# Layer 3's cross pass: output matrix as two float32r parts in products of 512 columns, and a new task order

## The chip, the cores and the metric

One core of one Trainium2 chip. The metric is the device time of one launch in microseconds, the median of several runs. In this profile TensorE is PE (its weight loads PEld), VectorE is DVE, ScalarE is ACT, GpSimd is POOL, SyncE is SP.

## What is computed

A four-layer network on X of 16 batches x 128 tokens x 256 features, each layer an attention and a feed-forward part. Only layer 3's attention is touched. It has two passes, one over the batch's own tokens ("own") and one over a context ("cross"), and both do this (shortened from the reference; `wproj` has 2 x 2048 rows, half for each pass):

```
q = _ln(fp8_linear(ln_out, wqx, ...).reshape(b, s, g, hpg, d), qxln_w, qxln_b)
k, v = cond @ w_kv_x.T, split;  k = _ln(k, kxln_w, kxln_b)
o = _gqa(q, k, v)                      # 16 heads of 128, softmax over 128 keys
y = fp8_linear_pertensor(o * smooth, wproj)
x = x + y
```

The output projection rounds its input to FP8 values first. These have few bits, so they are exact in bfloat16 and in float32r alike. The matrix `wproj` is full float32, and so it is cut into parts that add up to it.

## The kernel before

`Layer3Pass.run` (L2388) writes one pass for one batch as some 85 tasks, and `CROSS_ORDER` (L2363) is a hand-written list of them: (group, task, number). Each engine walks the list and issues only the tasks that are its own, in that order (`steps`, L2488). An engine is in order: a task that waits for a semaphore holds all that stand behind it. One walk of the list, a *step*, works on four batches at once: group "a" (attention and output) on batch b, "c" (centre and turn heads) on b+1, "p" (project) on b+2, "r" on b+3. There are 14 walks with all or nearly all groups, two without "p", of which the last has "a" alone, and three shorter ones ahead that fill the pipeline.

The tasks of group "a", for units u = 0 to 3 of four heads each, and their engines:

- scores (PE, L2650) into the only score tile `s_ps`; maximum (DVE, L2860) reads it; exponential (ACT, L2723) reads it again and frees it; scores u+1 waits for exponential u.
- normalise (DVE, L2864), turn (PE, L2663), turned (ACT, L2757), apply (PE, L2670), scale (ACT, L2762).
- round (DVE, L2873): five instructions over 128x512, all bfloat16. The last, L2882, writes `catq`.
- output (PE, L2678): for each of four heads three products of 128x256, the heads' `catq` stationary, one for each bfloat16 part of the matrix (`wparts`), all added up in `o_ps[:, 0:256]`.
- add (DVE, L2884), once a batch: X += o_ps * scale.

Group "p": project 0 to 5 (PE, `product` L2597, float32r, 512 columns), keep (ACT, L2733), statistics (DVE, L2830), and at the end deviation (DVE, L2835) and inverse (POOL, L2546), which give mean and inverse deviation. Deviation waits until POOL has centred the batch before. Group "c": project and keep values (PE, ACT), center (POOL, L2554, four heads each, five of the six units), center here (DVE, L2852, the sixth), turn 0 to 5 (PE, L2632), affine (ACT, L2746).

The three bfloat16 parts are cut once, in the pass's fill (`cut_output`: ACT L2776, DVE L2894): four casts on ACT and four subtractions on DVE, by turns.

```
for p in range(PARTS):                                                    # L2686
    mm = nc.tensor.matmul(o_ps[:, 0:D], catq[:, u % 2, h, :], wparts[:, p, 4 * u + h, :], ...)
...
v.tensor_tensor(flat(catq[:, u % 2, :, :]), c16, m, ALU.subtract).then_inc(catq_ready, 1)   # L2882
```

Of the kernel before, what the change touches and what calls it, by code (L numbers as in the profile page):

```python
# [22 lines left out]
P = 128  # L23
# [2306 lines left out]
class Layer3Pass:  # L2330
# [35 lines left out]
        ("r", "value", 0), ("a", "scores", 1), ("a", "maximum", 1), ("c", "keep values", 1), ("a", "turn", 0),  # L2366
        ("a", "exponential", 1), ("c", "center here", 2), ("p", "project", 0), ("p", "keep", 0),
# [20 lines left out]
    def run(self):  # L2388
# [7 lines left out]
        with Stage(nc, self.name) as st:  # L2396
# [31 lines left out]
            weights = sb("weights", [P, 2, 4, P])  # L2428
            probst = sb("probst", [P, 2, 4, P])
# [3 lines left out]
            catq = sb("catq", [P, 2, 4, P], BF16)  # L2433
            wparts = sb("wparts", [P, PARTS, 16, D], BF16)
# [79 lines left out]
            with nc.Block() as block:  # L2514
# [72 lines left out]
                def _(pe):  # L2587
# [90 lines left out]
                    def output(b, u):  # L2678
                        pe.wait_ge(catq_ready, at_batch(b, U, u + 1))
                        if u == 0:  # L2680
                            wait(pe, added, at_batch(b, 1, 0))
                            if b == 0:

                                pe.wait_ge(part_left, 4)
                        for h in range(4):
                            for p in range(PARTS):  # L2686
# [13 lines left out]
                def _(act):  # L2700
# [45 lines left out]
                    def affine_task(b, m):  # L2746
                        if isinstance(b, int) and b == 0 and m == 0:

                            act.wait_ge(part_left, 4)
# [26 lines left out]
                    def cut_output():  # L2776
                        act.wait_ge(wproj_in, 16)
                        for p in range(2):
# [22 lines left out]
                def _(dve):  # L2801
# [82 lines left out]
                    def add(b, k):  # L2884
                        dve.wait_ge(multiplied, at_batch(b, U, U))
                        v.scalar_tensor_tensor(cols(self.X, b), o_ps[:, 0:D], out_scale[:, 0:1], cols(self.X, b),
                                               ALU.mult, ALU.add).then_inc(added, 1)
# [6 lines left out]
                    def cut_output():  # L2894
                        for p in range(2):
# [183 lines left out]
```

## Time and profile before

| | |
|---|---|
| median of 3 runs | 3121.82 us (3118.33 to 3124.68) |
| the profiled execution | 3118.86 us, its span 3117.0 us |
| mean granted TensorE clock | 0.886 of full |
| cross pass of layer 3 | from 2103.0 us (first DMA) to 2576.4 us |
| busy in the span | PE 2380.8 us, DVE 1739.0, ACT 1320.1, POOL 1169.4 |

Busy is the union of an engine's instructions. A PE product goes on for a while after the next has begun, so its busy time covers short stalls; DVE instructions also overlap a little at their ends, and between dependent ones lies a short pipeline gap that counts as neither busy nor, in the timeline, as a wait. The number in brackets at the end of a timeline row is the idle time before it, and what ended it.

### The profile page before, as it was taken

The page shows a single profiled execution, that of the slowest core. Times are in us where ns is not written, and L with a number is a line of the kernel's source. Part 1 is how long each engine was busy: PE and PEld are TensorE (multiplying, and loading weights), DVE is VectorE, ACT ScalarE, POOL GpSimd, SP SyncE. Part 2 cuts the span into 40 slices and gives each one's busy share as a digit, 9 for nine tenths or more (in the row PEclk, how much of TensorE's full clock was granted, in tenths as well). Part 3 has the DMA queues.
Part 4 walks back from the last instruction along what each step waited for, and adds up shares of the span by engine and source line. Part 5 has one row for each costly group of instructions (what it writes and reads, how often), then busy time and mean ns, then how long its engine had stood idle before and what let it go on. Part 6 is the DMA issues. An engine that isn't in the chain of part 4 may idle for free. (4 is left out here: it accounts for less than half of the span.)

```text
span 3117.0 us, 45806 instructions
## 1 busy us (share of the span) xinstructions
PE 2380.8 (76%) x14906; PEld 1740.0 (56%) x14906; DVE 1739.0 (56%) x3738; ACT 1320.1 (42%) x3059; POOL 1169.4 (38%) x1183
## 2 busy tenths in 40 slices
PE   4887043955988577479558888877999983999997
PEld 2332022433546333367447777766888873777876
DVE  4775585645444155233368888866888864233232
ACT  0667151740200145211167777765788761111110
POOL 4541003510002242130167777736888851500000
PEclk9999565986989789789779999988999986999999
DMA  5232102532210323200110000011000001200001
GB/s 124 69 86 57 39 0 71 152 101 101 115 53 0 69 66 90 66 18 1 35 61 1 0 0 0 1 41 39 5 5 5 2 1 75 59 1 1 1 1 27
DMA packets 85673, 127.72 MB, mean 41 GB/s; under 512 B 20203, under 2 KB 66827, under 8 KB 81803
## 3 DMA queue, kind: packets, MB, share of 16 engines
q1 hardware_dynamic: 85515, 125.67, 14.1%
q8 instruction: 92, 1.51, 0.2%
q14 instruction: 66, 0.54, 0.1%
HBM read 75.99 MB, written 11.14 MB: 28 GB/s over the span
## 5 line engine op out<-in xcount | busy, mean ns | idle before, releaser
L478 DVE TENSOR_REDUCE a_mraw<-a_first_ps 128x4 f32<-128x1024 f32 (+1 forms) x256 | 310.7, 1222 | 148.0 <-PE a_first_ps L329 147.6
L386 ACT ACTIVATE a_et<-a_second_ps 128x1024 f32<-128x1024 f32 x256 | 262.1, 1024 | 160.6 <-PE a_second_ps L347 158.4
L2558 POOL TENSOR_SCALAR a3x_raw<-a3x_raw,a3x_mu,a3x_dev 128x128 f32<-128x128 f32 x320 | 281.7, 892 | 5.3 <-issue 5.3
L1451 DVE TENSOR_TENSOR f3e_gated<-f3e_silu,f3e_u_ps 128x512 f32<-128x512 f32 x96 | 66.1, 688 | 304.1 <-PE f3e_s_ps L1402 299.2
L2558 POOL TENSOR_SCALAR a3o_raw<-a3o_raw,a3o_mu,a3o_dev 128x128 f32<-128x128 f32 x256 | 232.0, 917 | 4.8 <-issue 4.8
L1432 ACT ACTIVATE f3e_silu<-f3e_g_ps 128x512 f32<-128x512 f32 x96 | 57.4, 598 | 396.1 <-PE f3e_g_ps L1389 396.1
L1411 PE MATMUL f3e_y_ps<-f_w,f3e_hidden 128*128 128x256 f32 x768 | 181.4, 380 | 0.0
L364 PE MATMUL a_o_ps<-a_et,a_vt 128*32 128x256 f32 x2048 | 168.0, 400 | 7.3 <-ACT a_osb L416 6.1
L347 PE MATMUL a_second_ps<-a_qs,a_ks 64*128 64x256 bf16 (+2 forms) x896 | 117.8, 298 | 63.7 <-ACT a_et L386 54.1
L1411 PEld LDWEIGHTS f3e_y_ps<-f_w,f3e_hidden 128*128 128x128 f32 x768 | 146.6, 191 | 18.4 <-DVE f3e_hidden L1454 1.2
L329 PE MATMUL a_first_ps<-a_ks,a_qs 64*128 64x256 bf16 (+2 forms) x1280 | 123.6, 268 | 19.1 <-DMA a_ks<-a_parts 10.4
L347 PEld LDWEIGHTS a_second_ps<-a_qs,a_ks 64*128 64x128 bf16 (+1 forms) x896 | 42.0, 96 | 163.2 <-ACT a_et L386 127.9
L2728 ACT ACTIVATE a3x_weights<-a3x_s_ps,a3x_nmax 128x128 f32<-128x128 f32 x256 | 91.1, 377 | 60.4 <-DVE a3x_nmax L2862 60.4
L1371 POOL CAST f_w_high<-f_w_raw 128x512 fp32r<-128x512 f32 x36 | 25.0, 694 | 238.2 <-SPq L1350 220.3
L2728 ACT ACTIVATE a3o_weights<-a3o_s_ps,a3o_nmax 128x128 f32<-128x128 f32 x256 | 93.1, 412 | 27.5 <-DVE a3o_nmax L2862 27.1
L2549 POOL TENSOR_TENSOR a3o_dev<-a3o_var,a3o_minus_half 128x24 f32<-128x24 f32 x16 | 69.0, 4310 | 94.8 <-DVE a3o_var L2850 94.8
L1362 POOL CAST f_x_high<-f_xnt 128x1024 fp32r<-128x1024 f32 x9 | 9.3, 1038 | 252.7 <-PE f3e_s_ps L1402 175.1
L2687 PE MATMUL a3o_o_ps<-a3o_wparts,a3o_catq 128*128 128x256 bf16 x768 | 101.9, 286 | 0.6 <-DVE a3o_catq L2882 0.6
L2606 PE MATMUL a3x_p_ps<-a_wkv,a3x_ctx_parts 128*128 128x512 f32 x384 | 102.1, 409 | 0.0
L2606 PE MATMUL a3o_p_ps<-a_wq,a3o_xq 128*128 128x512 f32 x256 | 80.6, 441 | 27.5 <-ACT a3o_vv L2743 16.8
L329 PEld LDWEIGHTS a_first_ps<-a_ks,a_qs 64*128 64x128 bf16 (+1 forms) x1280 | 72.0, 101 | 45.8 <-issue 16.1
L2687 PE MATMUL a3x_o_ps<-a3x_wparts,a3x_catq 128*128 128x256 bf16 x768 | 94.2, 273 | 0.7 <-DVE a3x_catq L2882 0.7
(537 smaller groups left out, 6380.4 us busy)
## 6 DMA issues: line engine op xcount, KB each, us to landing
f_w<-in_f_w SPq DMA_DIRECT2D x16, 1216.0 KB, 8.5
a_qs<-a_parts SPq DMA_DIRECT2D x144, 128.0 KB, 2.4
a_ks<-a_parts SPq DMA_DIRECT2D x96, 128.0 KB, 2.4
f_w_raw<-in_f_w SPq DMA_DIRECT2D x25, 256.0 KB, 2.6
a_od<-a_osb SPq DMA_DIRECT2D x64, 64.0 KB
a_oc<-a_od SPq DMA_DIRECT2D x16, 256.0 KB, 2.8
a_zr<-a_zd SPq DMA_DIRECT2D x64, 64.0 KB
a_od<-a_osb SPq DMA_DIRECT2D x8, 512.0 KB, 3.3
```

What stands on the lines that cost most here:

```text
L329: last = nc.tensor.matmul(self.first_ps[:, g % 2, u, c * N:c * N + N], self.queries(p, self.ROWS, b, tq, rows), self.keys(p, self.ROWS, b, ...
L347: last = nc.tensor.matmul(out, self.keys(p, self.ROWS_WITH_MAXIMA, b, t, rows), self.queries(p, self.ROWS_WITH_MAXIMA, b, tq, slice(0, N)) ...
L364: last = nc.tensor.matmul(self.o_ps[32 * j:32 * j + 32, columns], self.vt[:, b // 2 % self.NV, b % 2, c, self.block(k, j), :], self.et[:, ...
L386: self.nc.scalar.activation(self.et[:, g % self.WAVES_HELD, :, :], self.second_ps[:, :, :], ACT.Exp, scale=self.scale).then_inc(self.e_rea ...
L478: v.tensor_reduce(out, self.first_ps[:, g % 2, :, :].rearrange("p u (c n) -> p u c n", n=N), AX.X, ALU.max).then_inc(self.max_taken, 1)
L1411: last = nc.tensor.matmul(y_ps[:, k, 0:D], hidden[:, t % 2, k * P:k * P + P], self.w2[:, t, :], start=(t == 0), stop=(t == L - 1))
L1451: nc.vector.tensor_tensor(gated[:, t % 2, :], silu[:, t % 2, :], u_ps[:, :], ALU.mult).then_inc(gated_ready, 1)
L2549: nc.gpsimd.tensor_tensor(dev[:, :], var[:, :], minus_half[:, :], ALU.pow)
L2558: mm = nc.gpsimd.tensor_scalar(head, head, mu[:, h:h + 1], dev[:, h:h + 1], ALU.subtract, ALU.mult)
L2606: mm = nc.tensor.matmul(out, lhs, rhs, start=(i == 0), stop=(i == len(pairs) - 1))
L2687: mm = nc.tensor.matmul(o_ps[:, 0:D], catq[:, u % 2, h, :], wparts[:, p, 4 * u + h, :], start=(u == 0 and h == 0 and p == 0), stop=(u == U ...
L2728: mm = nc.scalar.activation(weights[:, u % 2, h, :], s_ps[:, h, :], ACT.Exp, bias=nmax[:, u % 2, h:h + 1], accum_out=total[:, u % 2, h:h + 1])
```

## The change

In the cross pass alone (the own pass keeps its code):

- The matrix is kept as two float32r parts side by side, `whalves` (128 x 16 x 2 x 256), in place of `wparts` of three bfloat16 parts. ACT copies (rounds) it in two halves, DVE subtracts in two halves.
- `catq` becomes float32r. Its four other rounding tiles stay bfloat16.
- output: for each head one product of 512 columns, high part into `o_ps[:, 0:256]`, low part into `o_ps[:, 256:512]`.
- add: two additions to X, with a drain between them.
- `weights` and `probst` move into `wraw`, the buffer that the own pass loaded weights through, which is free by then.
- `CROSS_ORDER` is another.

```
-            catq = sb("catq", [P, 2, 4, P], BF16)
-            wparts = sb("wparts", [P, PARTS, 16, D], BF16)
+            catq = sb("catq", [P, 2, 4, P], BF16 if own else F32R)
+            if own:
+                wparts = sb("wparts", [P, PARTS, 16, D], BF16)
+            else:
+                whalves = sb("whalves", [P, 16, 2, D], F32R)
+            LEFT = 4 if own else 2
...
                         for h in range(4):
+                            if not own:
+                                mm = nc.tensor.matmul(o_ps[:, :], catq[:, u % 2, h, :],
+                                                      whalves[:, 4 * u + h, :, :].rearrange("p k n -> p (k n)"),
+                                                      start=(u == 0 and h == 0), stop=(u == U - 1 and h == 3))
+                                continue
...
                     def cut_output():
                         act.wait_ge(wproj_in, 16)
+                        if not own:
+                            for h in range(2):
+                                nc.scalar.copy(whalves[:, 8 * h:8 * h + 8, 0, :], wproj[:, 8 * h:8 * h + 8, :]
+                                               ).then_inc(part_taken, 1)
+                            return
...
                     def add(b, k):
                         dve.wait_ge(multiplied, at_batch(b, U, U))
+                        if not own:
+                            v.scalar_tensor_tensor(cols(self.X, b), o_ps[:, D:2 * D], out_scale[:, 0:1], cols(self.X, b),
+                                                   ALU.mult, ALU.add)
+                            v.drain()
                         v.scalar_tensor_tensor(cols(self.X, b), o_ps[:, 0:D], out_scale[:, 0:1], cols(self.X, b),
                                                ALU.mult, ALU.add).then_inc(added, 1)
...
                     def cut_output():
+                        if not own:
+                            for h in range(2):
+                                dve.wait_ge(part_taken, h + 1)
+                                v.tensor_tensor(whalves[:, 8 * h:8 * h + 8, 1, :], wproj[:, 8 * h:8 * h + 8, :],
+                                                whalves[:, 8 * h:8 * h + 8, 0, :].bitcast(F32),
+                                                ALU.subtract).then_inc(part_left, 1)
+                            return
```

What the new list does to the engines is seen best in a step written out behind the loop. POOL's and SP's rows are the same before and after.

PE, from the first output task (`o_ps`) of a step to the second scores (`s_ps`) of the next. Here `t_ps` is a turn of four heads, `av_ps` apply, `p_ps` with `ctx_parts` projection of keys or values. Before:

```order
L2687 MATMUL a3x_o_ps<-a3x_wparts,a3x_catq 128x256 x12
L2674 MATMUL a3x_av_ps<-a3x_probst,a3x_vv 128x256 x2
L2687 MATMUL a3x_o_ps<-a3x_wparts,a3x_catq 128x256 x12
L2647 MATMUL a3x_t_ps<-a3x_ident,a3x_raw 128x128 x8
L2687 MATMUL a3x_o_ps<-a3x_wparts,a3x_catq 128x256 x12
L2647 MATMUL a3x_t_ps<-a3x_ident,a3x_raw 128x128 x4
L2687 MATMUL a3x_o_ps<-a3x_wparts,a3x_catq 128x256 x12
L2659 MATMUL a3x_s_ps<-a3x_qk 128x128 x4
L2606 MATMUL a3x_p_ps<-a_wkv,a3x_ctx_parts 128x512 x12
L2659 MATMUL a3x_s_ps<-a3x_qk 128x128 x4
```

After:

```order
L2694 MATMUL a3x_o_ps<-a3x_whalves,a3x_catq 128x512 x4
L2654 MATMUL a3x_t_ps<-a3x_ident,a3x_raw 128x128 x4
L2681 MATMUL a3x_av_ps<-a_wraw,a3x_vv 128x256 x2
L2694 MATMUL a3x_o_ps<-a3x_whalves,a3x_catq 128x512 x4
L2654 MATMUL a3x_t_ps<-a3x_ident,a3x_raw 128x128 x8
L2694 MATMUL a3x_o_ps<-a3x_whalves,a3x_catq 128x512 x4
L2654 MATMUL a3x_t_ps<-a3x_ident,a3x_raw 128x128 x8
L2694 MATMUL a3x_o_ps<-a3x_whalves,a3x_catq 128x512 x4
L2666 MATMUL a3x_s_ps<-a3x_qk 128x128 x4
L2613 MATMUL a3x_p_ps<-a_wkv,a3x_ctx_parts 128x512 x12
L2666 MATMUL a3x_s_ps<-a3x_qk 128x128 x4
```

Twelve products of 256 columns are four of 512, and one turn moved behind the third output task. Ahead of these rows, the other applies and projections stand earlier than before.

DVE, from the add of a batch over maximum 0, normalise 0 and so on to the statistics of units 0 and 1. Before:

```order
L2886 SCALAR_TENSOR_TENSOR X<-a3x_o_ps,a3x_out_scale,X 128x256
...
L2862 TENSOR_REDUCE a3x_nmax<-a3x_s_ps 128x4
L2866 RECIPROCAL a3x_inv_total<-a3x_total 128x4
L2869 TENSOR_TENSOR a3x_weights<-a3x_weights,a3x_inv_total 128x512
L2862 TENSOR_REDUCE a3x_nmax<-a3x_s_ps 128x4
L2857 TENSOR_SCALAR a3x_raw<-a3x_raw,a3x_mu,a3x_dev 128x128 x4
L2866 RECIPROCAL a3x_inv_total<-a3x_total 128x4
L2869 TENSOR_TENSOR a3x_weights<-a3x_weights,a3x_inv_total 128x512
L2862 TENSOR_REDUCE a3x_nmax<-a3x_s_ps 128x4
L2833 BN_STATS a3x_stats<-a3x_raw 128x6 x8
```

After:

```order
L2904 SCALAR_TENSOR_TENSOR X<-a3x_o_ps,a3x_out_scale,X 128x256
L2907 SCALAR_TENSOR_TENSOR X<-a3x_o_ps,a3x_out_scale,X 128x256
...
L2879 TENSOR_REDUCE a3x_nmax<-a3x_s_ps 128x4
L2883 RECIPROCAL a3x_inv_total<-a3x_total 128x4
L2886 TENSOR_TENSOR a_wraw<-a_wraw,a3x_inv_total 128x512
L2879 TENSOR_REDUCE a3x_nmax<-a3x_s_ps 128x4
L2874 TENSOR_SCALAR a3x_raw<-a3x_raw,a3x_mu,a3x_dev 128x128 x4
L2883 RECIPROCAL a3x_inv_total<-a3x_total 128x4
L2886 TENSOR_TENSOR a_wraw<-a_wraw,a3x_inv_total 128x512
L2879 TENSOR_REDUCE a3x_nmax<-a3x_s_ps 128x4
L2850 BN_STATS a3x_stats<-a3x_raw 128x6 x8
```

Nothing is moved in this stretch; one addition is new.

DVE, later in the step, from the end of round 0 to the start of the next one. Before:

```order
L2882 TENSOR_TENSOR a3x_catq<-a3x_cat,a3x_cmagic 128x512
L2866 RECIPROCAL a3x_inv_total<-a3x_total 128x4
L2869 TENSOR_TENSOR a3x_weights<-a3x_weights,a3x_inv_total 128x512
L2833 BN_STATS a3x_stats<-a3x_raw 128x6 x4
L2268 TENSOR_SCALAR a3x_cat<-a3x_cat 128x512
```

After:

```order
L2899 TENSOR_TENSOR a3x_catq<-a3x_cat,a3x_cmagic 128x512
L2850 BN_STATS a3x_stats<-a3x_raw 128x6 x8
L2883 RECIPROCAL a3x_inv_total<-a3x_total 128x4
L2886 TENSOR_TENSOR a_wraw<-a_wraw,a3x_inv_total 128x512
L2268 TENSOR_SCALAR a3x_cat<-a3x_cat 128x512
```

Statistics 3 and 4 now stand ahead of normalise 3, and rounds 1, 2 and 3 follow on each other with nothing between them (before, statistics 4 stood between rounds 1 and 2).

## Rows read from the trace of the kernel before

**Rows 1.** Window of 27 us in the middle of the cross pass.

```profile
core 0: us, PE busy (x) PEld busy (x) DVE busy (x) ACT busy (x) POOL busy (x), PEclk, DMA share, GB/s
2300.00:2327.00 27.00, 26.98 (x182) 23.15 (x181) 21.81 (x70) 21.56 (x69) 22.95 (x24) 1.00 0.02 5
```

**Rows 2.** Timeline of PE in one step: start us, us, instructions.

```profile
2301.94 1.47 PE L2687 MATMUL a3x_o_ps<-a3x_wparts,a3x_catq 128*128 128x256 bf16 x12
2303.25 1.03 PE L2674 MATMUL a3x_av_ps<-a3x_probst,a3x_vv 128*128 128x256 f32 x4
...
2321.80 1.64 PE L2606 MATMUL a3x_p_ps<-a_wkv,a3x_ctx_parts 128*128 128x512 f32 x6
2323.27 1.03 PE L2674 MATMUL a3x_av_ps<-a3x_probst,a3x_vv 128*128 128x256 f32 x4
```

**Rows 3.** Timeline of DVE, one step from add to add (its waits).

```profile
2310.56 0.48 DVE L2886 SCALAR_TENSOR_TENSOR X<-a3x_o_ps,a3x_out_scale,X 128x256 f32 x1
...
2313.33 0.18 DVE L2866 RECIPROCAL a3x_inv_total<-a3x_total 128x4 f32<-128x4 f32 x1 [1.57 <-ACT a3x_weights L2728]
...
2314.54 0.69 DVE L2862 TENSOR_REDUCE a3x_nmax<-a3x_s_ps 128x4 f32<-128x512 f32 x1 [0.27 <-PE a3x_s_ps L2659]
...
2316.81 0.18 DVE L2866 RECIPROCAL a3x_inv_total<-a3x_total 128x4 f32<-128x4 f32 x1 [0.39 <-ACT a3x_weights L2728]
...
2318.02 0.69 DVE L2862 TENSOR_REDUCE a3x_nmax<-a3x_s_ps 128x4 f32<-128x512 f32 x1 [0.27 <-PE a3x_s_ps L2659]
...
2329.53 0.38 DVE L2268 TENSOR_SCALAR a3x_cat<-a3x_cat 128x512 bf16<-128x512 bf16 x1 [0.34 <-ACT a3x_cat L2767]
...
2332.14 0.41 DVE L2268 TENSOR_SCALAR a3x_cat<-a3x_cat 128x512 bf16<-128x512 bf16 x1 [0.32 <-ACT a3x_cat L2767]
...
2333.45 0.79 DVE L2878 TENSOR_TENSOR a3x_cat<-a3x_cat,a3x_cmagic 128x512 bf16<-128x512 bf16 x1
...
2335.70 0.20 DVE L2839 TENSOR_TENSOR a3x_mu<-a3x_stats 128x24 f32<-128x24 f32 x1 [0.16 <-issue]
...
2337.33 0.48 DVE L2886 SCALAR_TENSOR_TENSOR X<-a3x_o_ps,a3x_out_scale,X 128x256 f32 x1
```

**Rows 4.** Groups of DVE by line, cross pass (busy us, mean ns, idle before).

```profile
L2869 DVE TENSOR_TENSOR a3x_weights<-a3x_weights,a3x_inv_total 128x512 f32<-128x512 f32 x64 | 44.6, 697 | 4.8
L2882 DVE TENSOR_TENSOR a3x_catq<-a3x_cat,a3x_cmagic 128x512 bf16<-128x512 bf16 x64 | 29.1, 454 | 4.8
```

**Rows 5.** Groups of DVE by shape, whole span: a subtraction with mixed types, one without.

```profile
L1747 DVE TENSOR_TENSOR f0h_scaled<-f0h_scaled,f0h_magic 128x2048 f32<-128x2048 f32 x8 | 18.3, 2292 | 0.6
L1750 DVE TENSOR_TENSOR f0h_hid<-f0h_scaled,f0h_magic 128x2048 bf16<-128x2048 f32 x8 | 18.3, 2292 | 0.8
```

**Rows 6.** Timeline of POOL in one step.

```profile
2288.76 17.80 POOL L2558 TENSOR_SCALAR a3x_raw<-a3x_raw,a3x_mu,a3x_dev 128x128 f32<-128x128 f32 x20 [0.19 <-issue]
2306.54 0.78 POOL L2576 TENSOR_TENSOR a3x_ctx_parts<-a3x_ctxs,a3x_ctx_parts 128x256 fp32r<-128x256 f32 x1
2310.65 4.19 POOL L2549 TENSOR_TENSOR a3x_dev<-a3x_var,a3x_minus_half 128x24 f32<-128x24 f32 x1 [3.33 <-DVE a3x_var L2850]
```

**Rows 7.** Timeline of DVE and POOL in the pass's fill.

```profile
2121.83 4.53 DVE L2899 TENSOR_TENSOR a3x_qk<-a3x_qk,a3x_wparts 128x2048 f32<-128x2048 f32 x2
2126.28 4.52 DVE L2899 TENSOR_TENSOR a3x_wparts<-a3x_qk,a3x_wparts 128x2048 bf16<-128x2048 f32 x2
...
2122.00 6.16 POOL L2549 TENSOR_TENSOR a3x_dev<-a3x_var,a3x_minus_half 128x24 f32<-128x24 f32 x1 [11.63 <-DVE a3x_var L2850]
...
2128.84 17.60 POOL L2558 TENSOR_SCALAR a3x_raw<-a3x_raw,a3x_mu,a3x_dev 128x128 f32<-128x128 f32 x20 [0.19 <-issue]
```

**Rows 8.** Timeline of PE: scores 0 and 1 of the first step and of the last two.

```profile
2147.41 1.92 PE L2659 MATMUL a3x_s_ps<-a3x_qk 128*128 128x128 f32 x8
...
2522.45 1.06 PE L2659 MATMUL a3x_s_ps<-a3x_qk 128*128 128x128 f32 x8
...
2550.42 1.06 PE L2659 MATMUL a3x_s_ps<-a3x_qk 128*128 128x128 f32 x8
```

More of the change, by code:

```diff
@@ L2365 @@
         ("c", "keep values", 0), ("a", "normalise", 0), ("c", "center", 0), ("c", "project values", 1),
-        ("r", "value", 0), ("a", "scores", 1), ("a", "maximum", 1), ("c", "keep values", 1), ("a", "turn", 0),
-        ("a", "exponential", 1), ("c", "center here", 2), ("p", "project", 0), ("p", "keep", 0),
[14 rows of a table removed]
+        ("r", "value", 0), ("a", "scores", 1), ("a", "maximum", 1), ("c", "keep values", 1), ("p", "project", 0),
+        ("a", "exponential", 1), ("c", "center here", 2), ("a", "turn", 0), ("p", "keep", 0), ("a", "normalise", 1),
[14 rows of a table added]
     ]
@@ L2427, in run @@
             inv_total = sb("inv_total", [P, 2, 4])
-            weights = sb("weights", [P, 2, 4, P])
-            probst = sb("probst", [P, 2, 4, P])
+            if own:
+                weights = sb("weights", [P, 2, 4, P])
+                probst = sb("probst", [P, 2, 4, P])
+            else:
+                weights, probst = (mats.wraw[:, k, :].rearrange("p (u h n) -> p u h n", u=2, h=4) for k in range(2))
             cat16 = sb("cat16", [P, 2, 4, P], BF16)
@@ L2432, in run @@
             cmagic = sb("cmagic", [P, 4, P], BF16)
-            catq = sb("catq", [P, 2, 4, P], BF16)
-            wparts = sb("wparts", [P, PARTS, 16, D], BF16)
+            catq = sb("catq", [P, 2, 4, P], BF16 if own else F32R)
+            if own:
+                wparts = sb("wparts", [P, PARTS, 16, D], BF16)
+            else:
+                whalves = sb("whalves", [P, 16, 2, D], F32R)
+            LEFT = 4 if own else 2
             wproj = qk[:, :, :, :].rearrange("p h k n -> p (h k n)")[:, 0:16 * D].rearrange("p (k n) -> p k n", k=16)
@@ L2682, in output @@
                             if b == 0:
-                                pe.wait_ge(part_left, 4)
+                                pe.wait_ge(part_left, LEFT)
                         for h in range(4):
+                            if not own:
[3 more added lines that the diff above has]
+                                continue
                             for p in range(PARTS):
@@ L2747, in affine_task @@
                         if isinstance(b, int) and b == 0 and m == 0:
-                            act.wait_ge(part_left, 4)
+                            act.wait_ge(part_left, LEFT)
                         act.wait_ge(heads_turned, at_batch(b, L, m + 1))
```

28 rows, old and new, of the table CROSS_ORDER are left out of this document.

## Prediction

> **What bounds the kernel now.** I read four views of the cross pass: windows, PE's timeline, DVE's timeline with the waits in it, and POOL's timeline. Only this pass changes. From scores 0 of its first step to scores 0 fourteen steps later pass 2522.45 - 2147.41 = 375.0 us, so a step takes 26.8 us [rows 8].
>
> The window [rows 1] seems to answer at once: PE is busy 26.98 of 27 us at full granted clock (2.4 GHz), weight loads 23.15, DVE 21.8, ACT 21.6, POOL 23. But PE's busy time includes the tail of each product, so a stall of a few tenths does not show in it. The reader should therefore ask a second question of each engine: if PE were free at once, how short could a step be? For DVE the timeline answers it [rows 3]. From add to add pass 26.77 us, and the waits in between are seven: 1.57 (normalise 0 for exponential 0), 0.27 (maximum 1 for scores 1), 0.39 (normalise 1 for exponential 1), 0.27 (maximum 2 for scores 2), 0.34 and 0.32 (rounds 2 and 3 for ACT's scale), 0.16 (deviation). Sum 3.32. All the rest, 23.45 us, is DVE's own work with its pipeline gaps.
>
> Four of these waits are not PE's doing. There is one score tile: maximum u, exponential u, scores u+1, maximum u+1 follow on each other, and DVE has nothing in its order to put in the holes but what is there now. 1.57 + 0.27 + 0.39 + 0.27 = 2.50 us stay however fast PE becomes. With the 0.16 that makes a ring through DVE of 23.45 + 2.66 = 26.11 us. Before the change DVE is thus within 0.66 us a step of being the bound: PE can give back two waits, 0.34 + 0.32, and no more.
>
> POOL's ring is shorter: 4.19 for the power, about 0.7 to the first centre (as in the fill, from 2128.16 to 2128.84), 17.80 for twenty centres [rows 6, 7], and DVE's deviation 2337.33 - 2335.70 = 1.63 [rows 3]: 24.3 us. It waits 3.33 us for DVE.
>
> **The change part by part, for a step.**
>
> Output products. An output task holds PE from 2301.94 to 2303.25, 1.31 us for twelve of 256 columns. A float32r product of 512 columns with a new stationary each time is there too: six take 2323.27 - 2321.80 = 1.47, so 0.245 each and four 0.98 [rows 2]. PE is relieved of 4 x (1.31 - 0.98) = 1.32 us a step. On the path lies of this only what DVE waited for, at most 0.66.
>
> Task order. On PE, applies and projections stand earlier, so ACT's scale is earlier. On DVE the stretch from add to the statistics of units 0 and 1 is the same, so the four waits of 2.50 remain. Later, rounds 1, 2, 3 stand together behind normalise 3, with two statistics ahead of it: 1.6 us of work that moved in front. Both let the scales be ready when the rounds come. I take the whole 0.66 as gained. The bound from below for this term is 0 (the waits stay), and nothing else in DVE's order is removed.
>
> The second addition. It reads PSUM like the present one: 0.48, and with the drain that holds the next about 0.56 [rows 3]. It stands at DVE's worst place: maximum 0 is queued behind it, exponential 0 waits for that, scores 1 for this, and with it PE. Nothing covers it: +0.56. Nothing in the timeline would let it be less.
>
> `catq` as float32r. This is a side effect of the type, four times a step: a subtraction of two bfloat16 tiles of 128x512 that writes 32-bit values. No row shows this mixture. The nearest below is the present one, all bfloat16: 0.43 in the timeline's rounds, mean 454 ns with a few held up. The nearest above is the same operation at the same width in float32: 0.69, mean 697 ns [rows 4]. What do mixed types take? At 2048 elements, a float32 subtraction takes 2292 ns with float32 output and 2292 with bfloat16 output [rows 5]: one 16-bit operand does not help where others are 32-bit. By this I take the upper end, 0.69, +0.26 each and +1.04 a step. The lower end is 0. The Trainium skill says the same of the unseen case: by "VectorE: DVE Perf Modes", section "What auto-detection actually checks", two elements a cycle need every tensor of a two-source operation to be 16-bit. If a 16-bit source were enough, against that page, this term would be nothing.
>
> So DVE's ring: 26.77 - 0.66 + 0.56 + 1.04 = **27.71 us**, +0.94 against now. PE then needs about 26.8 - 1.32 = 25.5 at most, POOL 24.3: both wait for DVE. PE will stand still behind scores 0 and the value projections until exponential 0 is done, about 1 us longer than now, and again ahead of some outputs for `catq`.
>
> Weight loads for 32-bit `catq` are longer than for bfloat16, but the 0.245 above is start to start with such loads. The move of `weights` and `probst` costs nothing: same shapes, same types, no wait added.
>
> Number of steps. Fourteen steps run at DVE's ring. The first is an exception: the clock is low at its start, and its scores take 1.92 instead of 1.06 us [rows 8], so PE holds part of it; I count it half. 13 x 0.94 + 0.5 = **+12.7**.
>
> The last two steps. In the one from 2522.45 to 2550.42 (27.97 us) the projections are absent. It ends on POOL's last centre (about 22.6 us after deviation's result) and then on output tasks behind turns. The new order puts only one turn and one output task, 0.44 + 0.98, behind that centre, where two output tasks at 1.31 stood. I take -2.0, between 0 and -3. The very last step: shorter output, longer last `catq` and the second addition: -0.33 + 0.26 + 0.56, about **+0.4**.
>
> The fill. Four subtractions of 2.26 us on DVE become two [rows 7], and two of ACT's casts go. The path there is POOL's: power from 2122.00, centres until 2146.4, scores at 2147.41 [rows 7, 8]. The power took 6.16 us beside the subtractions, 4.19 in the loop [rows 6]. With half of them gone I take **-0.7** (0 to -2.0). DVE's and ACT's other savings are covered by POOL's centres.
>
> Sum: 12.7 - 2.0 + 0.4 - 0.7 = **+10.4 us**. The profiled execution of 3118.86 would become 3129.3 (its span is 1.9 less). The median of the runs is 3.0 above that execution, so the median forecast is 3121.82 + 10.4 = **3132 us**.
>
> **The rivals.**
>
> 1. *PE is the bound, and DVE's holes shrink with it.* For it speaks the 26.98 of 27. Against it speak the four waits above, which end on ACT and on scores that were issued as soon as ACT was done. It would give -1.32 x 14 = -18.5, with the ends some -21: 3101 us. It decides if a step is nearer 25.5 than 26.8. The Trainium skill (its first page, "Trainium Kernel Development and Optimization", section "Performance Expectations") warns against reading matmul busy time as nearness to the limit; the weight loads, 23.15 of 27, agree with the warning. Chance 0.06.
>
> 2. *`catq` costs no more than now.* Then the ring is 26.77 - 0.66 + 0.56 = 26.67, -0.1 a step: -1.4, and with the ends' -2.0 + 0.1 - 0.7 it is -4: 3118 us. Deciding point: the mean duration of the last instruction of a round, 0.45 against 0.69. Chance 0.13.
>
> 3. *The order's gain does not come, or DVE and POOL get in each other's way.* A bfloat16 sum at 2333.45 took 0.79 where others take 0.52 [rows 3], at the time at which POOL subtracts in `ctx_parts` (26.64 us after 2306.54 [rows 6]). If such a meeting falls on every step anew it is +0.3 x 14 = +4. If the two waits of 0.66 remain it is +0.66 x 13 = +9. Together up to 3144, each alone 3136 to 3141. Chance 0.17.
>
> 4. *The change shortens nothing on PE*, since a product with both operands new runs at 0.3 or more. PE would still be at 26.7 and hidden by DVE's 27.7: the forecast's time. No chance of its own.
>
> **How the numbers follow.** A difference under 0.2% (6.2 us) can hardly be told from none here. The forecast, 0.64, spans about +4 to +15, from the bounds of its small terms; about a sixth of it lies under +6.2. Rival 2 has most of its chance within 0.2%, a little below. So: faster 0.09, same 0.21, slower 0.70. The range takes in the forecast, most of rival 2 and the single cases of rival 3: 3118 to 3140.
>
> **What would show it.** In the profile after: the last instruction of round at 0.69 instead of 0.43; two additions of 0.48; add to add 27.7 us; no wait of DVE for ACT's scale; still 1.57 ahead of normalise 0; PE's busy time at 25 to 26 of 27 with waits named ahead of scores 1 and output; POOL's wait ahead of its power grown from 3.3 to above 4 us. The prediction is wrong if a step is under 26.7 us: then either `catq` was cheap (its row tells), or the four waits did move with PE.

## The result and the profile after

The changed kernel takes 3130.69 us (median of 14 runs, 3123.89 to 3135.19), the kernel before 3122.82 (median of 14, 3118.33 to 3127.28). The ratio is 1.0025, 95% interval 1.0016 to 1.0033: 5 to 10 us slower. The profiled execution took 3130.35 us.

First the page's head. Beside before's numbers in the table above, PE has lost 12 us of busy time and DVE has gained 13.

```profile
span 3128.6 us, 44810 instructions
...
PE 2369.1 (76%) x14394; PEld 1712.2 (55%) x14394; DVE 1751.8 (56%) x3752; ACT 1316.7 (42%) x3057; POOL 1181.1 (38%) x1183
```

The window of one step in the middle of the pass, to be read beside [rows 1]:

```profile
2311.00:2338.00 27.00, 25.70 (x144) 20.97 (x144) 22.41 (x71) 20.89 (x68) 23.51 (x23) 1.00 0.02 5
```

PE was busy 26.98 of 27 us and now 25.70, at the same full clock: in equal windows it is busy 1.3 us less. A step is not such a window, since it has become longer. From add to add (mean of 13) PE's busy time falls from 26.52 to 25.79 us, by 0.73, and its idle time grows from 0.11 to 1.56. Where PE stands still is in its timeline of that step, in every step at the same two places: ahead of the last output task and ahead of scores 1.

```profile
2311.28 1.20 PE L2694 MATMUL a3x_o_ps<-a3x_whalves,a3x_catq 128*128 128x512 f32 x4 [0.59 <-DVE a3x_catq L2899]
2312.31 1.05 PE L2666 MATMUL a3x_s_ps<-a3x_qk 128*128 128x128 f32 x8
2313.12 3.04 PE L2613 MATMUL a3x_p_ps<-a_wkv,a3x_ctx_parts 128*128 128x512 f32 x12
2317.06 1.16 PE L2666 MATMUL a3x_s_ps<-a3x_qk 128*128 128x128 f32 x8 [0.90 <-ACT a_wraw L2740]
```

Output at 512 columns goes start to start in 1.03 us a task (2312.31 - 2311.28), where 1.31 was [rows 2] and 0.98 forecast.

DVE from add to add, the counterpart of [rows 3]:

```profile
2309.99 1.24 DVE L2899 TENSOR_TENSOR a3x_catq<-a3x_cat,a3x_cmagic 128x512 fp32r<-128x512 bf16 x1
...
2313.70 0.48 DVE L2904 SCALAR_TENSOR_TENSOR X<-a3x_o_ps,a3x_out_scale,X 128x256 f32 x1
2314.27 0.48 DVE L2907 SCALAR_TENSOR_TENSOR X<-a3x_o_ps,a3x_out_scale,X 128x256 f32 x1
2314.77 0.69 DVE L2879 TENSOR_REDUCE a3x_nmax<-a3x_s_ps 128x4 f32<-128x512 f32 x1
2317.04 0.18 DVE L2883 RECIPROCAL a3x_inv_total<-a3x_total 128x4 f32<-128x4 f32 x1 [1.57 <-ACT a_wraw L2740]
...
2318.25 0.69 DVE L2879 TENSOR_REDUCE a3x_nmax<-a3x_s_ps 128x4 f32<-128x512 f32 x1 [0.27 <-PE a3x_s_ps L2666]
...
2320.52 0.18 DVE L2883 RECIPROCAL a3x_inv_total<-a3x_total 128x4 f32<-128x4 f32 x1 [0.50 <-ACT a_wraw L2740]
...
2321.74 0.69 DVE L2879 TENSOR_REDUCE a3x_nmax<-a3x_s_ps 128x4 f32<-128x512 f32 x1 [0.16 <-PE a3x_s_ps L2666]
...
2328.03 0.70 DVE L2899 TENSOR_TENSOR a3x_catq<-a3x_cat,a3x_cmagic 128x512 fp32r<-128x512 bf16 x1
...
2332.74 0.70 DVE L2899 TENSOR_TENSOR a3x_catq<-a3x_cat,a3x_cmagic 128x512 fp32r<-128x512 bf16 x1
...
2335.05 0.70 DVE L2899 TENSOR_TENSOR a3x_catq<-a3x_cat,a3x_cmagic 128x512 fp32r<-128x512 bf16 x1
...
2337.35 1.24 DVE L2899 TENSOR_TENSOR a3x_catq<-a3x_cat,a3x_cmagic 128x512 fp32r<-128x512 bf16 x1
...
2341.07 0.48 DVE L2904 SCALAR_TENSOR_TENSOR X<-a3x_o_ps,a3x_out_scale,X 128x256 f32 x1
```

The reader should see four things. The wait of 1.57 ahead of normalise 0 stands as it was. Both waits for ACT's scale are gone. The last instruction of a round takes 0.70 and not 0.43. And one of the four takes 1.24. POOL's timeline tells what that one met:

```profile
2309.96 0.72 POOL L2583 TENSOR_TENSOR a3x_ctx_parts<-a3x_ctxs,a3x_ctx_parts 128x256 fp32r<-128x256 f32 x1
2313.78 4.18 POOL L2556 TENSOR_TENSOR a3x_dev<-a3x_var,a3x_minus_half 128x24 f32<-128x24 f32 x1 [3.10 <-DVE a3x_var L2867]
...
2318.91 18.44 POOL L2565 TENSOR_SCALAR a3x_raw<-a3x_raw,a3x_mu,a3x_dev 128x128 f32<-128x128 f32 x20 [0.57 <-issue]
2337.32 0.72 POOL L2583 TENSOR_TENSOR a3x_ctx_parts<-a3x_ctxs,a3x_ctx_parts 128x256 fp32r<-128x256 f32 x1
```

POOL's subtraction in `ctx_parts` starts at 2309.96 and 2337.32, DVE's slow `catq` at 2309.99 and 2337.35. Over the pass, the group of [rows 4]:

```profile
L2899 DVE TENSOR_TENSOR a3x_catq<-a3x_cat,a3x_cmagic 128x512 fp32r<-128x512 bf16 x64 | 51.2, 800 | 5.1 <-issue 0.4
```

**Where the time went.** I measure the pass from add to add.

| us | before | after | difference | forecast |
|---|---|---|---|---|
| pass start to the first add | 74.34 | 71.34 | -3.0 | -0.7 + 0.5 |
| 13 steps | 13 x 26.626 | 13 x 27.346 | +9.4 | +12.2 |
| last step but one | 27.11 | 25.16 | -1.95 | -2.0 |
| last step and what follows it | 25.79 | 27.16 | +1.4 | +0.4 |
| the pass | 473.4 | 479.2 | +5.8 | +10.4 |

The two profiled spans differ by 11.6 us, the pass by 5.8; the rest lies in stages that the change does not touch (the pass itself starts 2.2 us later). The medians differ by 7.9. The experiments below were each timed against the kernel before on the same chip (its medians there: 3122.57 for e1 to e4, 3123.30 for e5 to e7, 3123.53 for e8 to e10), and the pass of each was also measured in its trace, which leaves out the stages that no edit touches. One of e8's eleven runs took 5506.66 us, in a slow state, and is not in its ratio.

DVE's step, taken start to start over eight steps in the middle and grouped: additions 0.45 to 1.07; `catq` 1.55 to 3.02; the two scale waits, 0.65, gone; the other four instructions of a round, with statistics, maximum and centre, 0.85 less in all; everything else, the four waits that stay among it, 0.1 more. Sum 0.62 + 1.48 - 0.65 - 0.85 + 0.1 = +0.70, beside +0.71 over the same eight steps and +0.72 over 13.

### The profile page after: what moved, and what is told of

It is laid out like the page before. It is cut to its first block and busy times, and to the rows that moved or that the text cites. A ratio compares the mean times of both kernels' runs of the same rounds, so it can differ in the third digit from the quotient of the medians.

```text
span 3128.6 us, 44810 instructions
## 1 busy us (share of the span) xinstructions
PE 2369.1 (76%) x14394; PEld 1712.2 (55%) x14394; DVE 1751.8 (56%) x3752; ACT 1316.7 (42%) x3057; POOL 1181.1 (38%) x1183
## 5 line engine op out<-in xcount | busy, mean ns | idle before, releaser
L2565 POOL TENSOR_SCALAR a3x_raw<-a3x_raw,a3x_mu,a3x_dev 128x128 f32<-128x128 f32 x320 | 295.3, 935 | 5.3 <-issue 5.3
L329 PE MATMUL a_first_ps<-a_ks,a_qs 64*128 64x256 bf16 (+2 forms) x1280 | 122.1, 266 | 19.9 <-DMA a_ks<-a_parts 10.2
L2740 ACT ACTIVATE a_wraw<-a3x_s_ps,a3x_nmax 128x128 f32<-128x128 f32 x256 | 90.7, 368 | 76.0 <-DVE a3x_nmax L2879 76.0
L2666 PE MATMUL a3o_s_ps<-a3o_qk 128*128 128x128 f32 x512 | 74.3, 290 | 22.4 <-ACT a3o_weights L2740 21.6
```

The source lines that it names most:

```text
L329: last = nc.tensor.matmul(self.first_ps[:, g % 2, u, c * N:c * N + N], self.queries(p, self.ROWS, b, tq, rows), self.keys(p, self.ROWS, b, ...
L2565: mm = nc.gpsimd.tensor_scalar(head, head, mu[:, h:h + 1], dev[:, h:h + 1], ALU.subtract, ALU.mult)
L2666: mm = nc.tensor.matmul(s_ps[:, h, :], qk[:, q, 4 * u + h, :], qk[:, q, 16 + 2 * u + h // 2, :], start=True, stop=True)
L2740: mm = nc.scalar.activation(weights[:, u % 2, h, :], s_ps[:, h, :], ACT.Exp, bias=nmax[:, u % 2, h:h + 1], accum_out=total[:, u % 2, h:h + 1])
```

## The experiments

In each table row below: step is the mean of 13 steps add to add; "pass" its length.

| | median, ratio to before [95%] | pass | step |
|---|---|---|---|
| before | 3122.82 | 473.4 | 26.63 |
| after | 3130.69, 1.0025 [1.0016, 1.0033] | 479.2 | 27.35 |
| e1 order alone | 3124.92, 1.0007 [0.9998, 1.0016] | 472.5 | 26.61 |
| e2 products alone | 3133.32, 1.0038 [1.0027, 1.0050] | 482.7 | 27.34 |
| e3 one addition | 3121.45, 0.9999 [0.9990, 1.0008] | 469.0 | 26.70 |
| e4 half of `catq` | 3118.38, 0.9986 [0.9977, 0.9995] | 468.3 | 26.68 |
| e5 split moved | 3122.59, 0.9998 [0.9989, 1.0007] | 474.1 | 26.88 |
| e6 late additions | 3121.68, 0.9993 [0.9984, 1.0002] | 468.2 | 26.64 |
| e7 both | 3126.73, 1.0008 [0.9999, 1.0017] | 476.8 | 27.20 |
| e8 e6, last turn later | 3119.16, 0.9981 [0.9972, 0.9990] | 466.6 | 26.59 |
| e9 e8, split moved | 3116.56, 0.9977 [0.9968, 0.9986] | 466.6 | 26.51 |
| e10 e8 on old products | 3127.92, 1.0011 [1.0002, 1.0021] | 475.5 | 26.94 |

### e1: the new order on the old arithmetic

The kernel before, with the new `CROSS_ORDER`:

```
-        ("r", "value", 0), ("a", "scores", 1), ("a", "maximum", 1), ("c", "keep values", 1), ("a", "turn", 0),
+        ("r", "value", 0), ("a", "scores", 1), ("a", "maximum", 1), ("c", "keep values", 1), ("p", "project", 0),
...
```

> The kernel before with the new task list alone (bfloat16 parts, one addition). Theory (a ring through VectorE sets the step, and the order frees its two waits for the scales): the step falls from 26.66 us (add to add, mean of 13) to between 26.1, which is VectorE's ring without these waits, and 26.4, if TensorE's own work of some 26.0 us with small stalls takes over; time 3.5 to 8 us below before. Rival (TensorE is the bound and the products made the difference): no gain, 26.6 to 26.7, time within 2 us of before. Second rival (the order was only good together with short products): a longer step, 26.8 or more.

A miss: the step stays at 26.61, as before. Two scale waits of 0.34 and 0.32 have become one of 0.71, ahead of round 3 (DVE's timeline):

```profile
2334.37 0.43 DVE L2882 TENSOR_TENSOR a3x_catq<-a3x_cat,a3x_cmagic 128x512 bf16<-128x512 bf16 x1
2335.51 0.44 DVE L2268 TENSOR_SCALAR a3x_cat<-a3x_cat 128x512 bf16<-128x512 bf16 x1 [0.71 <-ACT a3x_cat L2767]
```

PE's idle time is 0.13 a step (0.11 in the kernel before). With two different orders PE has next to no idle time and the step is the same, so with twelve products PE is the limit, at 26.6, and DVE's scale waits are that limit as seen from DVE. What does come is 0.9 us in the step before the last.

### e2: the new products on the old order

The changed kernel, with the old `CROSS_ORDER` (the diff above the other way round).

> The changed kernel with the old task list. Theory: the ring through VectorE gets +0.57 for the second addition and +1.1 to +1.4 for the wider catq, and on the old list TensorE, relieved by 1.3 us, delivers the scales earlier too, so that most of the two waits goes without the new list: step 27.4 to 28.0, time 9 to 18 us above before. Rival (TensorE sets the step): 25.3 to 25.6, time 15 us or more below before. If the new list is what freed the waits, it is 27.9 or more; if not, within 0.2 of the changed kernel's 27.32.

The step is the changed kernel's to 0.01 us, and no scale wait is in it. So the products freed both waits and brought all of the loss per step, and the order brought nothing per step. The order is worth 3.5 us in the pass, at its end alone: the last step but one takes 27.04 here and 25.16 in the changed kernel, the last 27.89 against 26.12. `catq` has its 1.24 here too, once a step.

### e3: one addition

Each head's product split into two of 256 columns that add up in `o_ps[:, 0:256]`; the second addition and its drain go.

```
+                                for p in range(2):
+                                    mm = nc.tensor.matmul(o_ps[:, 0:D], catq[:, u % 2, h, :],
+                                                          whalves[:, 4 * u + h, p, :],
...
-                            v.scalar_tensor_tensor(cols(self.X, b), o_ps[:, D:2 * D], out_scale[:, 0:1], cols(self.X, b),
-                                                   ALU.mult, ALU.add)
-                            v.drain()
```

> The changed kernel with the two float32r parts summed in the same 256 columns of PSUM (eight products of 256 columns in each output task in place of four of 512) and so with one addition. Theory: the step loses the second addition, 0.57 us, and nothing else: 27.32 becomes 26.7 to 26.8, time about 8 us below the changed kernel, that is equal to before within 2 us; TensorE's output task may take up to 1.5 us with eight weight loads, and that must not show. Rival (TensorE matters): the longer output tasks give the gain back, step 27.2 or more.

The step loses 0.65, the pass 10.2 us. Eight products of 256 take PE no longer than four of 512:

```profile
2309.96 1.21 PE L2695 MATMUL a3x_o_ps<-a3x_whalves,a3x_catq 128*128 128x256 f32 x8 [0.58 <-DVE a3x_catq L2901]
```

The 0.65 is not the second addition alone. In this kernel POOL's subtraction meets `catq` 5 times in 64 and not 12, worth 0.27 a step over the eight middle steps; the additions take 0.54 less there, start to start; and other rows take 0.2 more. PE now waits for POOL's last centre, 1.1 us in every other step or 0.59 on the mean, where the changed kernel has no such wait.

So the wide product bought nothing here, and its price was the second addition. What PE gained, it gained from two float32r parts in place of three of bfloat16.

### e4: a shorter last instruction of round

The last instruction of a round writes 256 of the 512 columns, the rest of `catq` stays zero from the fill: half of the output projection is left out of the result. PE's work is the same.

```
-                        v.tensor_tensor(flat(catq[:, u % 2, :, :]), c16, m, ALU.subtract).then_inc(catq_ready, 1)
+                        n = 4 * P if own else 2 * P
+                        v.tensor_tensor(flat(catq[:, u % 2, :, :])[:, 0:n], c16[:, 0:n], m[:, 0:n],
+                                        ALU.subtract).then_inc(catq_ready, 1)
```

> The changed kernel, but the last instruction of a round writes the first 256 of 512 columns of catq alone; heads 2 and 3 of each unit stay zero, so half of the output projection is left out of the result, with all products still issued. Theory: the instruction takes about 0.42 us as the bfloat16 one did, in place of 0.69 and of 1.24 where it meets GpSimd's subtraction in ctx_parts, and the step loses 4 x 0.27 and some of the 0.54 of that meeting: 27.32 becomes 25.9 to 26.3, time 14 to 20 us below the changed kernel and 6 to 12 below before. Rival (the width of catq is covered by other waits): a step within 0.3 us of 27.3.

```profile
L2907 DVE TENSOR_TENSOR a3x_catq<-a3x_cat,a3x_cmagic 128x256 fp32r<-128x256 bf16 x64 | 27.8, 434 | 4.8
```

The instruction falls from 800 to 434 ns, four times a step 1.46, but the step falls by only 0.67. The sign is as expected, the size is missed: a scale wait of 0.50 a step is back ahead of a round's first instruction, and the neighbouring sum of two tiles takes 555 ns where it took 514. The trace shows why: POOL's subtraction now meets the sum, in 12 steps at 0.80 in place of 0.52.

```profile
2308.14 0.79 POOL L2588 TENSOR_TENSOR a3x_ctx_parts<-a3x_ctxs,a3x_ctx_parts 128x256 fp32r<-128x256 f32 x1
2308.41 0.80 DVE L2902 TENSOR_TENSOR a3x_cat<-a3x_cat,a3x_cmagic 128x512 bf16<-128x512 bf16 x1
```

DVE's relief counts until another limit is met, near 26.7 here as in e3. It need not be the same one: in e3 PE waits for POOL's centre, in e4 it never does. What holds e4's scale back no run tells.

### e5: POOL's split moved out of the way

POOL's subtraction into `ctx_parts` (task "quantise") is issued after the first centre and not at the end of the step.

```
-        ("c", "keep values", 0), ("a", "normalise", 0), ("c", "center", 0), ("c", "project values", 1),
+        ("c", "keep values", 0), ("a", "normalise", 0), ("c", "center", 0), ("r", "quantise", 0), ("c", "project values", 1),
```

> The changed kernel with one task moved on GpSimd: the subtraction in ctx_parts stands behind its first centre group, when VectorE does statistics, and no more behind the last, where VectorE writes catq of round 3. Theory (that meeting holds the catq instruction 1.24 instead of 0.70 us in nearly every second or each step): no catq over 0.8 us is left and the step goes from 27.35 to 26.8 to 27.0; time 5 to 8 us below the changed kernel. Rival (the long instruction is covered, or comes from something else): catq instructions over 1 us remain, step 27.2 or more.

```profile
L2899 DVE TENSOR_TENSOR a3x_catq<-a3x_cat,a3x_cmagic 128x512 fp32r<-128x512 bf16 x64 | 44.8, 701 | 5.1 <-issue 0.4
```

As expected: 701 ns, none above 1 us, step -0.47. This shows that the 1.24 was the meeting with POOL, and what it cost a step. Its price is on PE, which now waits 1.2 us a step for a centre, because the centres end later: POOL's timeline has 3.33 + 0.74 + 15.71 = 19.8 us from the first centre to the last, with the subtraction between, where it had 18.44.

```profile
2317.18 3.33 POOL L2565 TENSOR_SCALAR a3x_raw<-a3x_raw,a3x_mu,a3x_dev 128x128 f32<-128x128 f32 x4 [0.56 <-issue]
2320.49 0.74 POOL L2583 TENSOR_TENSOR a3x_ctx_parts<-a3x_ctxs,a3x_ctx_parts 128x256 fp32r<-128x256 f32 x1
2321.20 15.71 POOL L2565 TENSOR_SCALAR a3x_raw<-a3x_raw,a3x_mu,a3x_dev 128x128 f32<-128x128 f32 x16
```

And the wait in PE's:

```profile
2310.12 0.66 PE L2654 MATMUL a3x_t_ps<-a3x_ident,a3x_raw 128*128 128x128 f32 x4 [1.22 <-POOL a3x_raw L2565]
```

### e6 and e7: the additions into the hole

Both additions of a batch are issued behind maximum 0 of the next, where DVE waits 1.57 us for exponential 0. The first two steps are written out before the loop, since the first has nothing to add.

```
-        ("a", "scores", 0), ("a", "exponential", 0), ("a", "maximum", 0), ("c", "project values", 0),
+        ("a", "scores", 0), ("a", "exponential", 0), ("a", "maximum", 0), ("e", "add", 0), ("c", "project values", 0),
...
-        ("p", "deviation", 0), ("p", "inverse", 0), ("c", "affine", 4), ("c", "turn", 5), ("a", "add", 0),
+        ("p", "deviation", 0), ("p", "inverse", 0), ("c", "affine", 4), ("c", "turn", 5), 
```

> The changed kernel with the two additions moved behind maximum 0 of the next batch, into VectorE's wait of 1.57 us for exponential 0 (the first two steps are written out ahead of the loop). Theory (the ring is VectorE's, and 1.57 is a hole that nothing filled): both additions, 1.06 us with the drain, and a wait of 0.1 between them vanish from the ring: 27.35 becomes 26.2 to 26.4, time 12 to 15 us below the changed kernel. Rival (another chain is as long): the step stays above 26.6.

The step falls by 0.71 to 26.64, less than was expected, which is the rival's case (another chain is as long). A new wait in PE's timeline is a candidate for that chain; as in e3 it stands in about every other step, and is 0.53 on the mean of 13:

```profile
2332.11 0.65 PE L2661 MATMUL a3x_t_ps<-a3x_ident,a3x_raw 128*128 128x128 f32 x4 [1.16 <-POOL a3x_raw L2572]
2332.51 1.18 PE L2701 MATMUL a3x_o_ps<-a3x_whalves,a3x_catq 128*128 128x512 f32 x4
2333.53 1.05 PE L2673 MATMUL a3x_s_ps<-a3x_qk 128*128 128x128 f32 x8
```

The last turn waits for POOL's last centre, and output 3 and scores 0 are queued behind it. That would be a second ring: deviation, POOL's power and centres, last turn, output 3, scores 0, maximum 0, and from there through DVE's order to a later deviation. e7 is e6 with e5's move, which makes this ring longer:

> Both of the former moves in one kernel. Theory: 27.35 - 1.15 - 0.4 gives 25.7 to 26.0 a step, and with the shorter ends some 12 to 17 us below the kernel before: the ring through VectorE is then near TensorE's own 24.6 and GpSimd's 24.3, so that a part may be lost to them. Rival: a chain of waits that neither touches holds the step at 26.6, as the half-wide catq and the single addition both ended there; then e6 and e7 are alike and equal to before less the ends, 3 to 6 us below it.

It takes 27.20 a step, with 1.14 us of PE waiting for centres: outside the expected range and its rival's both. The two moves that each helped alone undo each other. So a later last centre does lengthen the step here; that this chain is what held e6 at 26.64 is not yet shown by it.

### e8 and e9: the last turn out of the way

The last turn and the last affine go behind scores 0 and exponential 1 of the next step; the rest is e6.

```
-        ("a", "scores", 0), ("a", "exponential", 0), ("a", "maximum", 0), ("c", "project values", 0),
+        ("a", "scores", 0), ("a", "turn last", 5), ("a", "exponential", 0), ("a", "maximum", 0), ("e", "add", 0), ("c", "project values", 0),
...
-        ("a", "exponential", 1), ("c", "center here", 2), ("a", "turn", 0), ("p", "keep", 0), ("a", "normalise", 1),
+        ("a", "exponential", 1), ("a", "affine last", 5), ("c", "center here", 2), ("a", "turn", 0), ("p", "keep", 0), ("a", "normalise", 1),
```

> The kernel with the late additions, and turn 5 and its affine moved from the end of a step behind scores 0 and behind exponential 1 of the next. Theory (a second ring of about 26.6 us runs from deviation over GpSimd's centres to turn 5, output 3, scores 0 and maximum 0, and held the late additions): scores 0 no longer wait for the last centre, the step goes from 26.64 to VectorE's ring of 26.2 or slightly under, 25.9 to 26.3; time 5 to 9 us below the kernel with the late additions, 7 to 10 below before. Rival (no such ring, the half microsecond was lost to slower VectorE instructions): 26.5 or more.

PE's wait for the centre is gone, yet the step is 26.59. By its own expectation that speaks for the rival (26.5 or more): taking the last centre out of scores 0's way brought 0.05 a step over 13, or 0.2 (26.67 to 26.46) over the eight in the middle. So the second ring explains at most a small part of what e6 missed. e9 adds e5's move, now with the centres off PE's path:

> The same, with GpSimd's subtraction in ctx_parts behind its first centre group too, where it made things worse (27.20) while turn 5 stood in front of scores 0. Theory: with the second ring opened the 0.78 us that it puts ahead of the later centres do no harm, and no catq instruction is held up any more: 25.6 to 26.0 a step, 2 to 6 us below the kernel without it. Rival (GpSimd's own ring of 24.3 to 25.9, with centres that grew to 19 us, now sets the step): 26.2 or more, no gain over the kernel without it.

The step is 26.51, a miss by half a microsecond at least, and again the rival's case (no gain over e8). The median is the lowest here, 3116.56 us, 0.9977 of before [0.9968, 0.9986], and 14 us under the changed kernel; but little tells it from e8: the intervals overlap, the pass is 466.6 in both, and the eight middle steps are 26.46 and 26.47. Of the 6.8 us that the pass is shorter than before's, the 13 steps give 1.5; 4.0 lie ahead of the first add and 1.3 behind the 13 steps. DVE's timeline of e9 at the old hole:

```profile
2307.01 0.69 DVE L2890 TENSOR_REDUCE a3x_nmax<-a3x_s_ps 128x4 f32<-128x512 f32 x1 [0.30 <-issue]
2307.61 0.47 DVE L2915 SCALAR_TENSOR_TENSOR X<-a3x_o_ps,a3x_out_scale,X 128x256 f32 x1
2308.17 0.48 DVE L2918 SCALAR_TENSOR_TENSOR X<-a3x_o_ps,a3x_out_scale,X 128x256 f32 x1
2309.27 0.18 DVE L2894 RECIPROCAL a3x_inv_total<-a3x_total 128x4 f32<-128x4 f32 x1 [0.61 <-ACT a_wraw L2749]
```

The wait of 1.57 is now 0.61. DVE still waits 2.11 us a step, in four to seven small pieces, and works 24.4; PE waits 0.85, of it 0.70 for `catq`; POOL waits 1.96 for DVE ahead of its power. Each has slack. I read it as DVE's ring again, with hand-overs of 0.2 to 0.6 between DVE, ACT and PE through the one score tile; no run here takes the tile's ring apart, so this stays open.

### e10: the same moves on the old products

> The same moves (new list, late addition, turn 5 behind scores 0) on the old arithmetic: three bfloat16 parts, one addition. Theory: here TensorE is the bound with 26.05 us of products, so the step is 26.1 to 26.4 whatever is freed elsewhere; the kernel with float32r products is below it by 0.1 to 0.4 a step and about 3 us at the ends. Rival (the bfloat16 version has the shorter VectorE ring, 25.6, and gets there): 25.6 to 25.9.

The step is 26.94, above the expected 26.1 to 26.4. PE is idle 0.15 of it and DVE waits 3.85: with twelve bfloat16 products PE holds the step, whatever DVE is spared. (Why PE needs 0.3 more here than in the kernel before, whose PE is idle 0.11, no run tells; its output tasks take the same 1.31.) Against e8 (26.59) the new products are worth 0.34 a step, once the second addition stands in a hole.

## Why the prediction was right

The forecast of 3132 us is 1.3 over the median, the case forecast (DVE's ring) is the one that came, and the range holds it. That it is as near as 1.3 is partly luck: the forecast stands on a before of 3121.82, which came out as 3122.82, and of the 7.9 between the medians only 5.8 is found in the pass, where 10.4 was forecast. Inside the step, too, errors cancelled. Point by point:

- **The bound.** DVE paces the changed step, PE is idle 1.56 us of it, and 1.57 stands unchanged ahead of normalise 0. The waits were as foretold: none for ACT's scale, new ones ahead of scores 1 and of an output. Rival 1 (PE is the bound, 3101) fell with these rows.
- **The four waits that stay.** 2.50 was forecast, 1.57 + 0.27 + 0.50 + 0.16 = 2.50 stands there.
- **Output products.** Relief 4 x 0.33 forecast, 4 x (1.31 - 1.03) = 1.12 by start to start. PE's busy time falls by 0.73 alone, since start to start the turns take 0.31 more a step and the projections of keys and values 0.26. I read that as short stalls, which busy time covers; no run shows it.
- **Task order: right in size, wrong in cause.** "I take the whole 0.66 as gained" came true, but e1 shows that the order alone gains none of it, and e2 that the products alone gain all. The text put the cause on rounds that stand later; the waits were PE's lateness, in either order. The forecast's 0.66 is thus right here by luck.
- **The second addition.** +0.56 forecast; 0.62 by start to start, and e3, which takes it away, gives back 0.65 (though not by this alone, see there).
- **`catq`: mis-sized.** At 0.69 each the term was right for 51 of 64, and rival 2 (454 ns stays, 3118) fell. But the forecast added 4 x 0.26 = 1.04 and it was 1.48: in 12 of the 16 steps the last of the four meets POOL's subtraction. It was rival 3's mechanism, priced at +0.3 a step and found at 0.54 for each meeting (1.24 - 0.70); e5 removes it and gains 0.47. The meeting itself is not new. The kernel before had it in the same twelve steps: seven times on the sum (0.79 in place of 0.52), four times on the bfloat16 `catq` (0.79 in place of 0.43), once on the instruction ahead of the sum (0.66 in place of 0.29). Here is POOL's side of the row at 2333.45 in [rows 3], and one of the four:

```profile
2333.18 0.78 POOL L2576 TENSOR_TENSOR a3x_ctx_parts<-a3x_ctxs,a3x_ctx_parts 128x256 fp32r<-128x256 f32 x1
...
2226.81 0.91 POOL L2576 TENSOR_TENSOR a3x_ctx_parts<-a3x_ctxs,a3x_ctx_parts 128x256 fp32r<-128x256 f32 x1
2227.21 0.79 DVE L2882 TENSOR_TENSOR a3x_catq<-a3x_cat,a3x_cmagic 128x512 bf16<-128x512 bf16 x1
```

The change moved it onto a longer instruction, so its net cost is 0.54 less the 0.27 to 0.37 that it cost already: about 0.2 a step.
- **What was not foreseen in the step.** Other instructions became shorter: the plain rounding operations 328 to 287 ns, exponents 344 to 316, the sum 530 to 514. With statistics, maximum and centre it is the 0.85 above, and without it the step would be near 28. The traces account for some 0.2 of it: the meeting with POOL, gone from the sum. The rest no experiment took apart. So 27.71 was forecast and 27.35 came, against a mean of 26.63 where the text had 26.77 from a single step: +0.72 against +0.94.
- **The move into `wraw`** was forecast at nothing. No run has it alone; normalise, which works on it, takes 702 ns against 697.
- **The last steps.** -2.0 forecast, -1.95 measured. By e2 against the changed kernel 1.9 of it is the order's (on the old products, e1, the order gives 0.9). The last stretch was forecast +0.4 and came out +1.4. It begins with the additions of the batch before and ends with its own, so it holds the second addition twice, and the text counted it once; in e3, without either, the stretch is 25.68 = 25.20 + 0.48, as before.
- **The fill: the wrong side of it.** -0.7 was looked for in the power, which stayed at 6.16: the two remaining subtractions still run beside it (that they are the cause, and not its being the first of the pass, no run shows). What got shorter are the centres, 17.60 [rows 7] to 15.68. Nearly all of it is the first of the twenty: in before it ran beside the last of DVE's subtractions (until 2130.80) and took 2.72, now it takes 0.95; the others take 0.79 in both, but for before's second (0.94). The first row is before's, the rest are the changed kernel's:

```profile
2128.84 2.72 POOL L2558 TENSOR_SCALAR a3x_raw<-a3x_raw,a3x_mu,a3x_dev 128x128 f32<-128x128 f32 x1 [0.19 <-issue]
...
2124.22 4.53 DVE L2919 TENSOR_TENSOR a3x_whalves<-a3x_qk,a3x_whalves 128x2048 fp32r<-128x2048 f32 x2
...
2124.39 6.16 POOL L2556 TENSOR_TENSOR a3x_dev<-a3x_var,a3x_minus_half 128x24 f32<-128x24 f32 x1 [11.68 <-DVE a3x_var L2867]
...
2131.11 15.68 POOL L2565 TENSOR_SCALAR a3x_raw<-a3x_raw,a3x_mu,a3x_dev 128x128 f32<-128x128 f32 x20 [0.19 <-issue]
```

Of the 3.0 that is 1.9. The first step gained the other 1.1, where +0.5 was forecast as if PE held half of it. In before's window 2147 to 2176 PE is busy 28.97 of 29 us at a granted clock of 0.91: it held all. (The same window after has 28.41 at 0.93, so the clock may have a part in it.)

The step terms were thus too high by 2.8 and the fill by 2.8, the last step too low by 1.0; the sum of 10.4 stands beside 5.8 in the pass and 7.9 by the medians.

## What to carry to other kernels

A busy share of 99.9% on one engine says little of how much it pays to relieve it: list the other engines' waits in one period and ask which of them that engine causes. Here that was 0.65 of 3.3 us, so relief of 1.1 us on PE could pay at most 0.65, and some 2 us of new work on DVE, the engine next to the limit, had to lose. The same arithmetic, with the additions in the period's longest wait, no longer costs anything in the step (e6: 26.64 against 26.63), and with the last turn moved as well the kernel is 0.2% under before (e8, e9), most of it at the ends of the pass. Removing a wait that the timeline names does not show that it was the limit: e8 took away the wait that seemed to hold e6, and the step hardly moved. And when an instruction is made longer, look at what it will run beside: the same meeting with POOL cost 0.27 on the sum and 0.54 on the 32-bit `catq`.

## What the runs showed of the hardware

- A subtraction of two bfloat16 tiles that writes 32-bit values takes what a float32 one takes: 0.70 us at 128x512, against 0.43 with a 16-bit result. By the Trainium skill ("VectorE: DVE Perf Modes", section "What auto-detection actually checks") a two-source operation takes its faster mode only if every tensor is 16-bit, and the trace agrees.
- This instruction took 1.24 in place of 0.70 when a two-source subtraction of POOL started 0.03 us before it, 12 times of 64; with POOL's instruction moved elsewhere none did (e5). The 0.54 is most of POOL's 0.72. With 16-bit results the meeting, in which POOL started 0.27 or 0.40 us earlier, cost 0.27 (sum, 0.52 to 0.79) or 0.36 (`catq`, 0.43 to 0.79).
- POOL's centres took longer in some company and not in other: twenty took 15.68 us in the changed kernel's fill, 17.80 in before's step [rows 6], 18.44 in the changed one, 18.69 in e8. What counts is which DVE instruction runs beside a centre, and not how busy DVE is: in the changed kernel a single one took 0.79 us beside DVE's statistics (36 of them, all 0.785 to 0.792), 0.84 to 0.91 beside a sum and the instruction ahead of it, and 1.42 to 1.46 where a 32-bit `catq` and the three instructions behind it ran in its time (29). In before's fill one took 2.72 beside a float32 subtraction of 128x2048.
- Two float32r products of 256 columns with one stationary take as long as one of 512 (1.04 us a task start to start for eight in e3, 1.03 for four in the changed kernel), though the stationary is loaded for each: 512 loads of 0.19 us in the pass in place of 256.
